# A decoder layer on one core: the second norm's rows in two halves, query units by token halves, and a new order of moves and stores

## The chip, the cores and the metric

The kernel runs on one core of a Trainium2 chip. The metric is the device time of one execution in microseconds (us); three runs of the kernel before gave a median of 809.94 us (808.97 to 810.89). About 0.2%, or 1.6 us, is what a measurement of this kernel can tell from no change.

## The reference, cut to what matters

Input x is 16 x 64 tokens of width 512, all in float32. Three steps follow each other, each with a residual:

```python
x = x + attn(layernorm(x))                    # scores over the 16 sequences, per channel; no weights
x = x + xattn(layernorm(x), ctx, mask, Wq, Wk, Wv, Wo, q_norm_w, k_norm_w)
        # 32 query heads of 128, 8 key/value heads: q = h @ Wq.T, k = ctx @ Wk.T, v = ctx @ Wv.T,
        # RMS norm of every q and k head, softmax(q k / sqrt(128) + mask) v, @ Wo.T
x = x + ffn(layernorm(x), ...)                # 16 experts, 4 per token, and a shared one
```

The change lies between the first and the second step: the second layer norm, the transposes of its rows, and the queries of the first of the eight head groups.

## The kernel before, in words

Every product is made of float16 halves: an operand is split into a high part (ScalarE, ACT, a copy to float16) and a low part (VectorE, DVE, or GpSimd, POOL, the difference), and TensorE (PE) adds high*high, high*low and low*high. So each result that feeds another product passes PE, ACT, then DVE or POOL, then PE again.

Time falls into a first stage (about the first 60 us: load x, first norm, attention over sequences), the eight head groups of the cross attention (about 62.7 us each once they run, to about 540 us) and the experts. A head group is software-pipelined: `iteration(i, att, proj)` does the attention of group i and the projections of group i+1. `iteration(-1, ...)`, the place of this change, has only projections: the queries of group 0, while keys and values of group 0 are made just before it. All order is written by hand; each engine works through its own list, and semaphores carry the waits.

Around the change, engine by engine:

- **DVE**: adds the first attention's result to x (L1238), takes statistics, computes the scale of each of 16 rows of 64 tokens (`row_scales`), then normalises 10 rows (L1193) while ACT normalises 6 (L751). Then 8 times `transposed_lo` (L1254), `v_lo_part` (L1264), and per query unit k of `iteration(-1)` a `q_lo_part` (L1279) and a `pre_lo` (L1364: low part of a 128x512 piece of expert weights, "units" 4 to 11). Between these stand `key_norm` (L1342, k = 1, 2), `key_lo` (L1348, k = 4, 5) and the second `v_lo_part` (k = 7).
- **ACT**: 8 times `transposed_hi` (L819), `v_hi_part` (L895), `k_scale(0)` (L877, L880), and per query unit `q_parts`: high part (L832), square (L836), high part of the square (L838), then `first_hi` (L924). `k_scale(1)` stands at k = 1, `k_hi_part` (L884) at k = 3, 4, the second `v_hi_part` at k = 7. After unit 7 come `wq_chunk` four times (L761), `q_rms` (L889, L891), which waits for the second half of the query squares' sums, `wkv_chunk`, four pairs of weight splits (L913, L915), and then `q_parts` of the next group.
- **PE**: first half of the values (L1742), 8 times `transpose_rows` (L1828, 4 transposes each), `sum_k_squares` (L1911, L1912), then 8 query units `project_q` of 12 products of 128x512; unit u is head u // 2 and token half u % 2. Unit u waits for `q_split` of unit u-2 (L1867), since two PSUM banks alternate. After unit 7 it computes the second half of the values (48 small products, 2.7 us), sums the query squares of the first token half (L1902, 32 products of one column) and goes on to group 0's scores (`scores`, L1844), which wait for all of `q_split` and for both `k_split` (L1847, L1848).
- **POOL**: `square_lo` per unit (L623), `k_square_lo` (L629), for which it waits until DVE's rows are normalised.
- **SyncE (SP)** issues the transfers: stores of split weights, second-round loads (L443), then four moves of x from one SBUF layout to another (L449), wq and wkv of group 1 (L421, L423), third-round loads (L402), stores of the second round (L416), wo (L460), stores of the third round, each followed by a load for group 1. `first_hi` of the third round (k = 4 to 7) waits on ACT for the store of the second round in the same slot (L922).

Of the kernel before, what the change touches and what calls it, by code (L numbers as in the profile page):

```python
# [18 lines left out]
ALU = mybir.AluOpType  # L19
# [55 lines left out]
DVE_ROWS = [n for n in range(B) if n not in ACT_ROWS]  # L75


def rows_to(rows, n):

    return sum(m <= n for m in rows)  # L80

# [12 lines left out]
def decoder_kernel(nc, x_half, ctx_t, mask, wq, wkv, wo, qk_norm, gate_t, bias, wgu, wd, h_rows, out):  # L94
    with ExitStack() as ctx:
# [292 lines left out]
        def _(sp):  # L388
# [55 lines left out]

            x_pairs = xh.rearrange("p (t b) l -> p t b l", b=2)
# [5 lines left out]
            query_weights(1)  # L451
            sp.wait_ge(hT_ps, NT)
            for q in range(SLOTS):
                sp.wait_ge(pre_in[q], 32)
                pre_load(0, 2 * SLOTS + q)
# [80 lines left out]
        def _(pool):  # L536
# [82 lines left out]
            def square_lo(p, u):  # L619
                j, th = u // 2, u % 2  # L620
# [53 lines left out]
            pool.wait_ge(h2_dve, len(DVE_ROWS))  # L674
# [52 lines left out]
        def _(act):  # L727
# [100 lines left out]
            def q_parts(p, u):  # L828
                j, th = u // 2, u % 2
# [87 lines left out]
            def first_hi(q):  # L917
# [3 lines left out]
                if n:  # L921
                    act.wait_ge(pre_stored[us], 16 * n)  # L922
# [15 lines left out]
            def iteration(i, att, proj, split):  # L938
# [4 lines left out]
                for k in range(8):  # L943
# [197 lines left out]
        def _(dve):  # L1141
# [43 lines left out]
            def normalise_rows(count, bank, dst, done):  # L1185
# [6 lines left out]
                for n in DVE_ROWS:  # L1192
                    dve.tensor_scalar(dst(n), xh[:, n, :], rstd[:, n:n + 1], shift_ln[:, n:n + 1],  # L1193
                                      ALU.mult, ALU.add).then_inc(done, 1)

            normalise_rows(1, 7, lambda n: hq[:, :, n], h1_dve)
# [73 lines left out]
            normalise_rows(2, 0, lambda n: h2[:, n, :], h2_dve)  # L1270
            for t in range(NT):
                transposed_lo(0, t, t % 4)
            v_lo_part(0, 0, 6)

            def q_lo_part(p, u):
                j, th = u // 2, u % 2
# [109 lines left out]
            def iteration(i, att, proj, split):  # L1386
# [4 lines left out]
                for k in range(8 if proj else 0):  # L1391
# [914 lines left out]
```

## Time and profile before

| what | value |
|---|---|
| runs shown | 808.97, 809.94, 810.89 us |
| profiled execution, its own time | 809.31 us |
| its span, first to last instruction | 807.5 us |
| PE busy | 777.2 us (96% of the span), 7887 matmuls |
| DVE, ACT, POOL busy | 591.6, 516.8, 543.3 us |
| mean granted TensorE clock | 0.993 |

A time line of the profile lists, for one engine, start, duration, line, output and inputs, count, and in brackets how long the engine stood idle before it and what released it. "x8" merges eight alike. Durations overlap the next start a little, since instructions are pipelined: a row of eight with 4.50 us is 0.56 us from start to start. PEclk 1.00 is the full 2.4 GHz, 0.50 is 1.2 GHz.

### The profile page before, as it was taken

What the parts mean: (1) busy time and instruction counts of PE and PEld (TensorE: products, weight loads), DVE (VectorE), ACT (ScalarE), POOL (GpSimd) and SP (SyncE); (2) the same over time, 40 slices, a digit from 0 to 9 for tenths busy, and PEclk for the clock granted to TensorE, in tenths of its full rate; (3) what the DMA queues carried; (4) which work ended last, traced back from release to release, by engine and by line L of the source; (5) the groups of instructions that cost most, each with busy time, mean ns of one, the idle gap of its engine ahead of it and who ended that gap; (6) DMA issues with size and microseconds to landing.
All of it is one profiled execution on the core that took longest, in us unless ns stands there. A gap on an engine that the chain in (4) does not pass through costs nothing.

```text
span 807.5 us, 21596 instructions
## 1 busy us (share of the span) xinstructions
PE 777.2 (96%) x7887; PEld 445.1 (55%) x7887; DVE 591.6 (73%) x1023; ACT 516.8 (64%) x968; POOL 543.3 (67%) x428
## 2 busy tenths in 40 slices
PE   6789999999999999999999999999998999999997
PEld 2664545645645655655654654654554565665653
DVE  5787795595685686777667668699688776767778
ACT  3898987487587587587578578636433566555551
POOL 6953496896896986976977978872253656565433
PEclk9799999999999999999999999999999999999999
DMA  8029516516507507516515524436515557678894
GB/s 329 18 95 290 164 67 235 143 53 227 165 26 234 164 18 238 168 36 229 158 55 188 176 79 151 124 113 248 177 52 209 199 182 248 219 282 277 264 401 183
DMA packets 50661, 138.94 MB, mean 172 GB/s; under 512 B 6176, under 2 KB 8224, under 8 KB 46240
## 3 DMA queue, kind: packets, MB, share of 16 engines
q1 hardware_dynamic: 43600, 116.93, 43.6%
q0 software_dynamic: 6400, 20.98, 7.6%
q8 instruction: 48, 0.79, 0.4%
q14 instruction: 21, 0.17, 0.1%
q10 hardware_dynamic: 592, 0.08, 0.1%
HBM read 96.02 MB, written 39.85 MB: 168 GB/s over the span
## 4 chain that ended last, share of the span: by engine, by line
PE 62%; POOL 13%; issue 8%; DVE 5%; DMA 5%; ACT 4%; SPq 2%; DVEq 0%; POOLq 0%; ACTq 0%
PE ps L1742 33%; PE ps L2192 18%; POOL ring_mem L623 4%; DMA stage<-in_wq 3%; POOL reg_h L661 3%; POOL ring_mem L609 2%; PE ps L2182 2%; POOL reg_h L665 2%; PE ps L1961 2%; POOL ring_mem L616 1%; PE ps L2253 1%; PE ps L1947 1%; PE ps L2207 1%; DMA w_split<-stage 1%; PE ps L1902 1%
## 5 line engine op out<-in xcount | busy, mean ns | idle before, releaser
L1742 PE MATMUL ps<-wo_hi,reg_b 128*128 128x512 f16 x448 | 142.5, 379 | 1.0 <-DVE x_res L1336 1.0
L2192 PE MATMUL ps<-ring_mem,reg_h 128*64 x480 | 116.6, 379 | 4.1 <-DVE kv L1639 2.3
L703 POOL DMA_INDIRECT y_rows<-reg_h,to_row x40 | 66.7, 1669 | 77.3 <-ACT reg_h L1115 71.6
L661 POOL TENSOR_SCALAR reg_h<-reg_h 128x512 f32<-128x512 f32 x56 | 95.4, 1704 | 33.2 <-ACT reg_h L913 33.0
L2194 PE MATMUL ps<-kv,reg_h 128*64 128x512 f16 x480 | 116.7, 380 | 0.0
L665 POOL TENSOR_TENSOR reg_h<-reg_h 128x512 f16<-128x512 f32 x84 | 108.7, 1294 | 4.7
L1742 PE MATMUL ps<-hT_hi,wq_hi 128*128 128x512 f16 x256 | 97.2, 380 | 2.0 <-DVE ring_mem L1279 1.8
L1742 PE MATMUL ps<-hT_hi,wq_lo 128*128 128x512 f16 x256 | 97.2, 380 | 0.0
L1742 PE MATMUL ps<-hT_lo,wq_hi 128*128 128x512 f16 x256 | 97.1, 379 | 0.0
L623 POOL TENSOR_TENSOR ring_mem<-kv,ring_mem 128x512 f16<-128x512 f32 x64 | 80.3, 1255 | 24.2 <-ACT ring_mem L838 24.2
L1742 PE MATMUL ps<-wo_lo,reg_b 128*128 128x512 f16 x224 | 85.0, 379 | 0.0
L2192 PEld LDWEIGHTS ps<-ring_mem,reg_h 128*64 128x64 f16 x480 | 48.3, 110 | 46.5 <-issue 15.0
L1742 PEld LDWEIGHTS ps<-wo_hi,reg_b 128*128 128x128 f16 x448 | 43.6, 97 | 50.8 <-issue 2.8
L1328 DVE TENSOR_TENSOR reg_b<-ps,reg_b 128x1024 f16<-128x1024 f32 x28 | 34.1, 1218 | 48.3 <-ACT reg_b L863 48.3
L1279 DVE TENSOR_TENSOR ring_mem<-ps,ring_mem 128x512 f16<-128x512 f32 x64 | 43.8, 685 | 29.0 <-ACT kv L836 28.3
L1336 DVE SCALAR_TENSOR_TENSOR x_res<-ps,x_res 128x512 f32<-128x512 f32 x64 | 43.7, 683 | 26.9 <-PE ps L1742 26.9
L913 ACT ACTIVATE reg_h<-reg_h 128x512 f16<-128x512 f32 x84 | 51.9, 620 | 11.6 <-DMA reg_h<-in_wgu 7.8
L2192 PE MATMUL ps<-ring_mem,wkv_st 128*64 x240 | 58.4, 379 | 0.9 <-ACT wkv_st L1107 0.8
L2194 PE MATMUL ps<-kv,wkv_st 128*64 128x512 f16 x240 | 58.4, 380 | 0.0
L609 POOL TENSOR_TENSOR ring_mem<-ring_mem,mask_sb 128x512 f32<-128x512 f32 x32 | 40.5, 1284 | 26.2 <-DVE ring_mem L1288 26.2
L699 POOL DMA_INDIRECT hT_hi<-h_rows,from_row x40 | 39.1, 979 | 19.7 <-issue 12.7
L832 ACT ACTIVATE ring_mem<-ps 128x512 f16<-128x512 f32 x64 | 38.1, 595 | 21.9 <-PE ps L1742 21.7
(343 smaller groups left out, 2019.2 us busy)
## 6 DMA issues: line engine op xcount, KB each, us to landing
ring_mem<-w_split SPq DMA_DIRECT2D x16, 1536.0 KB, 7.7
w_split<-reg_h SPq DMA_DIRECT2D x88, 256.0 KB, 2.1
reg_h<-in_wgu SPq DMA_DIRECT2D x58, 256.0 KB, 3.6
stage<-in_wq SPq DMA_DIRECT2D x8, 1024.0 KB, 8.9
stage<-in_wo SPq DMA_DIRECT2D x8, 1024.0 KB, 6.6
reg_h<-in_wd SPq DMA_DIRECT2D x30, 256.0 KB, 3.1
wkv_st<-in_wkv SPq DMA_DIRECT2D x8, 512.0 KB, 9.5
ring_mem<-in_x_half SPq DMA_DIRECT2D x8, 256.0 KB, 6.1
```

The source lines that it names most:

```text
L609: pool.tensor_tensor(t, t, mask_sb[:, :].unsqueeze(1).to_broadcast([P, 8, S]), ALU.add).then_inc(masked, 1)
L623: pool.tensor_tensor(sq_lo[:, j // 2, 8 * th:8 * th + 8, j % 2, :], sq32[:, u % 2, :].rearrange("p (b s) -> p b s", s=S), w, ALU.subtract) ...
L661: pool.tensor_scalar(st, st, WS, None, ALU.mult).then_inc(pre_scaled_pool, 1)
L665: pool.tensor_tensor(hl[:, 1, :], st, hl[:, 0, :], ALU.subtract).then_inc(pre_split, 1)
L699: pool.indirect_dma_start(h_slot[r % KC], None, h_rows, bass.IndirectOffsetOnAxis(ap=from_row[:, r - 1:r], axis=0)).then_inc(gathered[r % ...
L703: pool.indirect_dma_start(y_rows, bass.IndirectOffsetOnAxis(ap=to_row[:, r - 1:r], axis=0), y[r % 2], None).then_inc(scattered[r % 2], 16)
L913: act.activation(pre_hl[us][:, 0, :], pre_st[us], ACT.Copy, scale=WS).then_inc(pre_hi, 1)
L1279: dve.tensor_tensor(q_lo[:, j // 2, 8 * th:8 * th + 8, j % 2, :], ps[:, 4 + u % 2, :].rearrange("p (b s) -> p b s", s=S), q_hi[:, j // 2, ...
L1336: dve.scalar_tensor_tensor(x_res[:, t, :], ps[:, 2 + t % 2, :], 1.0 / (WS * WS), x_res[:, t, :], ALU.mult, ALU.add).then_inc(o_added, 1)
L1742: last = pe.matmul(dst, lhsT(c), rhs(c), start=(m == 0), stop=(m == n - 1))
L2192: pe.matmul(dst[0:TS, :], x[:, 0:TS], ring[:, bass.ds(at + w, BANK)], start=(first and n == 0), stop=(stop and n == 2))
L2194: last = pe.matmul(dst[TS:P, :], x[:, TS:P], upper_w[r % 2][:, w:w + BANK], start=(first and n == 0), stop=(stop and n == 2))
```

## The change

Rows of the second norm, their splits and transposes are taken in two halves of eight rows, with ACT and DVE going back and forth; PE computes the first query unit (head 0, first token half) between the two halves of the transposes; units of this group are then ordered (head 0, 1 of the first token half, head 0, 1 of the second, then heads 2 and 3 alike). The second half of the values, which ran after unit 7, is spread: one tile before the transposes, one after the first four, two after the last four. The sums of the key squares follow units 1 and 2. The key steps on ACT and DVE move to later units: `k_scale` to k = 2, 3, `key_norm` to 3, 4, `k_hi_part` to 5, 6, `key_lo` to 6, 7. SP issues group 1's wq and wkv and the third-round loads ahead of x's moves, and the third round's `first_hi` no longer waits for a store.

```diff
+SECOND_ACT_ROWS = ((1, 4, 6), (9, 12, 14))
+SECOND_DVE_ROWS = ((0, 2, 3, 5, 7), (8, 10, 11, 13, 15))
+def unit(p, u):
+    return (2 * (u // 4) + u % 2, u % 4 // 2) if isinstance(p, int) and p == 0 else (u // 2, u % 2)
...
# sync
+            query_weights(1)
+            sp.wait_ge(hT_ps, NT)
+            for q in range(SLOTS):
+                sp.wait_ge(pre_in[q], 32)
+                pre_load(0, 2 * SLOTS + q)
             x_pairs = xh.rearrange("p (t b) l -> p t b l", b=2)
             sp.wait_ge(x1_done, 8)
             ... four moves of x ...
-            query_weights(1)
-            sp.wait_ge(hT_ps, NT)
-            for q in range(SLOTS):
-                sp.wait_ge(pre_in[q], 32)
-                pre_load(0, 2 * SLOTS + q)
# gpsimd
-            pool.wait_ge(h2_dve, len(DVE_ROWS))
+            pool.wait_ge(h2_dve, len(SECOND_DVE_ROWS[0]))
# scalar
-                if n:
-                    act.wait_ge(pre_stored[us], 16 * n)
+                if n == 1:
+                    act.wait_ge(pre_stored[us], 16)
...
-                        if k == 1:
-                            k_scale(p, 1, 7)
-                        if k in (3, 4):
-                            k_hi_part(p, k - 3)
-                        if k == 7:
+                        if k in (2, 3):
+                            k_scale(p, k - 2, k - 2)
+                        if k in (5, 6):
+                            k_hi_part(p, k - 5)
+                        if k == 1:
                             v_hi_part(p, 1, 7)
...
-            normalise_rows(2, lambda n: h2[:, n, :], h2_act)
-            for t in range(NT):
-                transposed_hi(0, t, t % 4)
+            act.wait_ge(shift_ready, 2)
+            for part in range(2):
+                for n in SECOND_ACT_ROWS[part]:
+                    act.activation(h2[:, n, :], xh[:, n, :], ACT.Identity, scale=rstd[:, n:n + 1],
+                                   bias=shift_ln[:, n:n + 1]).then_inc(h2_act, 1)
+                for t in range(4 * part, 4 * part + 4):
+                    transposed_hi(0, t, t % 4)
             v_hi_part(0, 0, 6)
-            k_scale(0, 0, 7)
# vector: the same halves for its rows and transposed_lo, and
-                        if k in (1, 2):
-                            key_norm(p, k - 1)
-                        if k in (4, 5):
-                            key_lo(p, k - 4)
-                        if k == 7:
+                        if k in (3, 4):
+                            key_norm(p, k - 3)
+                        if k in (6, 7):
+                            key_lo(p, k - 6)
+                        if k == 1:
                             v_lo_part(p, 1, 7)
# tensor
+            def project_first_q():
+                pe.wait_ge(wq_split, KC)
+                pe.wait_ge(hT_hi_done, NT // 2)
+                ... for c in range(KC): wq_hi and wq_lo with hT_hi of the first half (8 products)
+                pe.wait_ge(hT_split, NT // 2)
+                ... for c in range(KC): wq_hi with hT_lo (4 products), then_inc(q_ps, 1)
...
-                            else:
-                                pe.wait_ge(hT_split, 4 * u + 4)
+                        if not att and u == 2:
+                            pe.wait_ge(hT_split, NT)
...
-                        project_q(p, u)
                         if not att and u == 0:
-                            pe.wait_ge(ln_k, 1)
-                            sum_k_squares(p, 1, 7)
+                            project_first_q()
+                            for t in range(NT // 2, NT):
+                                transpose_rows(t)
+                            project_v(0, 1, 7, range(2, 4))
+                        else:
+                            project_q(p, u)
+                        if not att and u in (1, 2):
+                            pe.wait_ge(hT_split, NT // 2 + u)
+                            sum_k_squares(p, u - 1, u - 1)
...
                     else:
-                        pe.wait_ge(ln_k, 2)
-                        project_v(p, 1, 7)
                         sum_q_squares(p, 3, range(NT // 2))
...
+            pe.wait_ge(x1_done, 4)
+            project_v(0, 1, 7, range(1))
             pe.wait_ge(var_ready, 2)
-            for t in range(NT):
+            for t in range(NT // 2):
                 transpose_rows(t)
-            sum_k_squares(0, 0, 7)
+            project_v(0, 1, 7, range(1, 2))
             iteration(-1, False, True)
```

## Rows read from the trace of the kernel before

**Rows 1.** The page's first part: busy time and share of each engine.
```profile
PE 777.2 (96%) x7887; PEld 445.1 (55%) x7887; DVE 591.6 (73%) x1023; ACT 516.8 (64%) x968; POOL 543.3 (67%) x428
```

**Rows 2.** Busy time in one stretch: us, busy us (instructions) per engine, PEclk, DMA share, GB/s.
```profile
300.00:400.00 100.00, 99.88 (x846) 55.55 (x844) 70.65 (x97) 70.68 (x125) 81.36 (x60) 1.00 0.51 162
```

**Rows 3.** PE in order of time: start, us, line, form, count [idle before <-releaser].
```profile
57.70 2.11 PE L1828 MATMUL ps<-ident,reg_h 128*128 128x128 f32 x16 [1.67 <-DVE reg_h L1193]
61.36 0.90 PE L1828 MATMUL ps<-ident,reg_h 128*128 128x128 f32 x5 [1.56 <-DVE hT_lo L1254]
...
84.29 0.39 PE L1742 MATMUL ps<-hT_hi,wq_hi 128*128 128x512 f16 x1 [0.83 <-DVE ring_mem L1279]
...
86.89 0.22 PE L1742 MATMUL ps<-wkv_hi,ring_mem 128*128 128x128 f16 x1
...
89.57 0.94 PE L1902 MATMUL ps<-ones,ring_mem 128*128 128x1 f16 x32
90.37 0.86 PE L1742 MATMUL ps<-kv,ring_mem 128*128 128x64 f16 x24
...
99.89 0.39 PE L1742 MATMUL ps<-hT_hi,wq_hi 128*128 128x512 f16 x1 [0.57 <-DVE ring_mem L1279]
```

**Rows 4.** ACT in order of time, second norm to the next head group; same columns.
```profile
56.95 3.06 ACT L751 ACTIVATE reg_h<-ring_mem,shift_ln,rstd 128x256 f32<-128x256 f32 x6 [0.31 <-DVE shift_ln L1189]
59.92 4.50 ACT L819 ACTIVATE hT_hi<-ps 128x512 f16<-128x512 f32 x8
...
64.79 0.69 ACT L877 ACTIVATE kv<-ps,eps_ln 128x512 f32<-128x512 f32 x1
...
66.84 0.60 ACT L832 ACTIVATE ring_mem<-ps 128x512 f16<-128x512 f32 x1 [0.70 <-PE ps L1742]
...
81.31 0.63 ACT L924 ACTIVATE reg_h<-reg_h 128x512 f16<-128x512 f32 x1 [1.49 <-DMA w_split<-stage]
...
87.09 0.60 ACT L832 ACTIVATE ring_mem<-ps 128x512 f16<-128x512 f32 x1 [0.32 <-PE ps L1742]
...
88.74 0.61 ACT L924 ACTIVATE reg_h<-reg_h 128x512 f16<-128x512 f32 x1
...
90.26 2.18 ACT L761 ACTIVATE wq_hi<-stage 128x512 f16<-128x512 f32 x4
92.34 0.27 ACT L889 ACTIVATE rq<-ps,eps_q 128x32 f32<-128x32 f32 x1
```

**Rows 5.** DVE in order of time, the same stretch.
```profile
56.95 3.32 DVE L1193 TENSOR_SCALAR reg_h<-ring_mem,rstd,shift_ln 128x256 f32<-128x256 f32 x10
60.53 4.88 DVE L1254 TENSOR_TENSOR hT_lo<-ps,hT_hi 128x512 f16<-128x512 f32 x8 [0.26 <-ACT hT_hi L819]
...
82.59 0.68 DVE L1348 TENSOR_TENSOR kv<-kv 128x512 f16<-128x512 f32 x1
...
88.28 0.69 DVE L1279 TENSOR_TENSOR ring_mem<-ps,ring_mem 128x512 f16<-128x512 f32 x1 [0.23 <-ACT kv L836]
89.39 1.23 DVE L1364 SCALAR_TENSOR_TENSOR reg_h<-reg_h 128x512 f16<-128x512 f32 x1 [0.42 <-ACT reg_h L924]
```

**Rows 6.** SyncE's queue in order of time: the four moves of x.
```profile
58.44 5.78 SPq L449 DMA_DIRECT2D x_res<-ring_mem  x4
```

**Rows 7.** Stretches with PE idle and the clock around them, columns as in rows 2.
```profile
21.31:23.18 1.87, 0.00 (x1) 0.00 (x0) 0.67 (x1) 1.31 (x2) 1.87 (x2) 1.00 0.03 13
...
24.90:28.30 3.40, 3.40 (x70) 2.78 (x71) 3.15 (x6) 2.44 (x5) 3.40 (x2) 0.50 0.00 0
32.93:36.18 3.25, 0.01 (x1) 0.04 (x1) 3.11 (x6) 3.15 (x7) 3.25 (x2) 0.84 0.00 0
...
35.10:41.95 6.85, 5.78 (x48) 5.81 (x50) 5.20 (x10) 6.36 (x11) 3.28 (x2) 0.50 0.01 4
...
610.60:613.15 2.55, 0.20 (x8) 0.04 (x3) 2.34 (x5) 1.08 (x3) 0.94 (x1) 1.00 0.55 231
```

**Rows 8.** PE in order of time, the longest stall between 200 and 500.
```profile
265.27 0.38 PE L1742 MATMUL ps<-wo_hi,reg_b 128*128 128x512 f16 x1 [0.71 <-DVE x_res L1336]
```

More of the change, by code:

```diff
@@ L75, with second_rows_to @@
 DVE_ROWS = [n for n in range(B) if n not in ACT_ROWS]
+SECOND_ACT_ROWS = ((1, 4, 6), (9, 12, 14))
+SECOND_DVE_ROWS = ((0, 2, 3, 5, 7), (8, 10, 11, 13, 15))
 def rows_to(rows, n):
     return sum(m <= n for m in rows)
+def second_rows_to(rows, n):
+    return max(i + 1 for i, m in enumerate(itertools.chain(*rows)) if m <= n)
+def unit(p, u):
+    return (2 * (u // 4) + u % 2, u % 4 // 2) if isinstance(p, int) and p == 0 else (u // 2, u % 2)
 def sums_to(t, k=None):
@@ L619, in square_lo @@
             def square_lo(p, u):
-                j, th = u // 2, u % 2
+                j, th = unit(p, u)
                 pool.wait_ge(sq_hi_done, ev(p, 8, u))
@@ L828, in q_parts @@
             def q_parts(p, u):
-                j, th = u // 2, u % 2
+                j, th = unit(p, u)
                 bank = ps[:, 4 + u % 2, :]
@@ L1183, in _, with row_shifts @@
             row_scales(1, 7)
-            def normalise_rows(count, bank, dst, done):
+            def row_shifts(count, bank):
                 dve.wait_ge(rstd_ready, count)
@@ L1191, in normalise_rows, with normalise_row @@
                 dve.wait_ge(shift_ready, count)
[L1192 to L1196, printed above, removed]
+            def normalise_row(n, dst, done):
+                dve.tensor_scalar(dst, xh[:, n, :], rstd[:, n:n + 1], shift_ln[:, n:n + 1],
+                                  ALU.mult, ALU.add).then_inc(done, 1)
+            row_shifts(1, 7)
+            for n in DVE_ROWS:
+                normalise_row(n, hq[:, :, n], h1_dve)
             dve.memset(used[:, 0:PRE], 1.0)
@@ L1269, in _ @@
             then(dve.tensor_tensor(wqk[:, :], norm_sb[:, 0:1], norm_sb[:, 1:2], ALU.mult))
-            normalise_rows(2, 0, lambda n: h2[:, n, :], h2_dve)
-            for t in range(NT):
-                transposed_lo(0, t, t % 4)
+            row_shifts(2, 0)
+            for part in range(2):
+                for n in SECOND_DVE_ROWS[part]:
+                    normalise_row(n, h2[:, n, :], h2_dve)
+                for t in range(4 * part, 4 * part + 4):
+                    transposed_lo(0, t, t % 4)
             v_lo_part(0, 0, 6)
             def q_lo_part(p, u):
-                j, th = u // 2, u % 2
+                j, th = unit(p, u)
                 dve.wait_ge(q_hi_done, ev(p, 8, u))
@@ L1819, in transpose_rows @@
             def transpose_rows(t):
-                pe.wait_ge(h2_dve, rows_to(DVE_ROWS, 2 * t + 1))
-                pe.wait_ge(h2_act, rows_to(ACT_ROWS, 2 * t + 1))
+                pe.wait_ge(h2_dve, second_rows_to(SECOND_DVE_ROWS, 2 * t + 1))
+                pe.wait_ge(h2_act, second_rows_to(SECOND_ACT_ROWS, 2 * t + 1))
                 if t >= 4:
@@ L1862, in project_q @@
             def project_q(p, u):
-                j, th = u // 2, u % 2
+                j, th = unit(p, u)
                 if u == 0:
@@ L1873, in project_q @@
                         range(KC)).then_inc(q_ps, 1)
+            def project_first_q():
+                pe.wait_ge(wq_split, KC)
+                pe.wait_ge(hT_hi_done, NT // 2)
+                for c in range(KC):
+                    for w in (wq_hi, wq_lo):
+                        pe.matmul(ps[:, 4, :], w[:, c, 0:HD], hT_hi[:, c, 0:BANK], start=(c == 0 and w is wq_hi), stop=False)
+                pe.wait_ge(hT_split, NT // 2)
+                for c in range(KC):
+                    last = pe.matmul(ps[:, 4, :], wq_hi[:, c, 0:HD], hT_lo[:, c, 0:BANK], start=False, stop=(c == KC - 1))
+                last.then_inc(q_ps, 1)
             def project_k(p, th):
@@ L2077, in _ @@
             project_v(0, 0, 6, range(2, 4))
+            pe.wait_ge(x1_done, 4)
+            project_v(0, 1, 7, range(1))
             pe.wait_ge(var_ready, 2)
-            for t in range(NT):
+            for t in range(NT // 2):
                 transpose_rows(t)
-            sum_k_squares(0, 0, 7)
+            project_v(0, 1, 7, range(1, 2))
             iteration(-1, False, True)
```

## The prediction

> **What bounds the kernel now.** I read the page's busy times first, then a table of busy time by stretches, then the time lines of PE, ACT, DVE and SyncE around the change. PE is busy for 777.2 of 807.5 us [rows 1] and for 99.88 of 100 us in the middle of the head groups [rows 2], so a microsecond that PE gains or loses before them arrives at the end almost whole. The longest stall between 200 and 500 us is 0.71 us [rows 8]. Ahead of the head groups PE does stand still: 1.67 us before the second norm's transposes, 1.56 us in the middle of them, 0.83 us before query unit 7, 0.57 us before unit 2 of the next group [rows 3]. The first two are what the halves are aimed at. The second thing to see is that ACT is as full there as PE: from 66.84, when it takes unit 0, to 87.09, when it takes unit 7, it idles for little but a 1.49 us wait for a store [rows 4]. Each query unit passes PE, ACT, DVE, and PE may run only two units ahead.
>
> **The change part by part.** Nothing moves before 56.95, when ACT and DVE begin their rows [rows 4, 5].
>
> *First half.* ACT takes 0.51 us a row (3.06 / 6) and 0.56 a high part (4.50 / 8) [rows 4]; DVE 0.33 a row and 0.61 a low part [rows 5]. After three rows ACT starts its four high parts at about 58.4; the last starts at 60.1 and PE sees it at 60.8. PE meanwhile does one value tile (0.67: a quarter of the 2.68 us between 86.89 and 89.57 [rows 3]), so its first stall shrinks from 1.67 to 1.1, then come the first 16 transposes from 57.7 (2.1 us [rows 3]) and another value tile, and waits 0.3 us. The first query unit runs from 60.8 to 63.4 instead of from 64.05.
>
> *Second half.* The last 16 transposes follow at 63.4 (they need DVE's row 15, ready at 63.2) and take 2.1 to 2.3 us, then two value tiles, 1.34: PE starts unit 1 at 67.0. It has most of its two stalls back, but has spent them on value tiles and on a unit that ACT cannot take yet. For ACT can make the second half's high parts only as the transposes come: it idles from 62.2 to 64.0, ends them at 66.4, does a value split, and **takes unit 0 at about 66.85, against 66.84 before** [rows 4]. This is the step that decides: the halves gain ACT nothing.
>
> *ACT from there to unit 7.* A unit with its weight split takes 1.65 + 0.52 = 2.17 us (87.09 to 88.74; 2.08 / 4) [rows 4]. Seven of them are 15.2. Both `k_scale` now lie here (before, one lay ahead of unit 0, at 64.79): about 1.3 each, 2.6. Two key high parts 1.0, one value split 0.5. Waits for PE: 0.8 before unit 1 (taken at 69.8, 2.8 after PE starts it), 0.4 before unit 2. The wait of 1.49 for the store [rows 4] is gone, since the third round has buffers of its own; the wait for its load replaces it at no cost, being issued at about 66, some 15 us ahead. Sum 20.5: unit 7 is taken at 87.3, against 87.09. The cover for all removed waits was ACT work, and that work is now the path.
>
> *After unit 7.* PE ends unit 7 at about 86.9 in both. Before, 2.68 us of values followed, then 0.8 us of sums, and the scores began at 90.37 without a stall [rows 3]. Now the values are used up. The scores need `q_split` of unit 7 and both `k_split`, and DVE has `key_lo(1)` last in its list, behind the weight split of k = 7, which waits for ACT's. From ACT's 87.3: 1.65 to its weight split (88.95), 0.65 to DVE's (88.74 to 89.39 [rows 4, 5]), 1.15 for that, about 0.75 for `key_lo` [rows 5]: the keys are ready at 91.5, or 91.3 with the shorter durations that these rows also allow. I take **91.4: PE stands still for about 3.6 us between 86.9 and 91.4, with 0.8 us of sums of one column in the middle, and starts the scores 1.0 us later than before.** ACT's `q_rms` needs the sums behind the first scores; it moves from 92.34 to about 93.1, +0.8, and with it the next group's first `q_parts`. There PE had 0.57 us of stall [rows 3], so its +1.0 is no more than ACT's +0.8. Net at this point: **+0.8**, between +0.3 (every DVE row at its shortest) and +1.2.
>
> *DVE and POOL share.* DVE's last weight split took 1.23 us [rows 5], while `key_lo`, of the same shape, took 0.68 with POOL idle. The Trainium skill (SBUF — State Buffer, "SBUF: two separate sides") has DVE operations with two SBUF inputs and POOL operations lock each other out for a whole instruction, and POOL's square split of unit 7 would still run there. By that rule the price is 1.23 again and the sum stays; without it the split would take 0.68 and the scores would come 0.5 us sooner, +0.3 to +0.5. The trace agrees with the rule, so I keep 1.23.
>
> *Queues.* SP issues group 1's wq and wkv at 58.4 instead of behind the 5.78 us of x's moves [rows 6]; neither is needed before 89. The third-round loads wait for the last transpose (65.7), the moves then run to about 73.5, and the second-round stores behind them start less than 1 us later. x's new place is first read after 94. I cost all of it at nothing; if a third-round load came late, ACT would wait again, at most the old 1.49. POOL's key squares start 1.6 us earlier, which nobody waits for.
>
> **The clock.** A stretch of some 4.4 us in which PE does only 0.8 us of one-column sums is new. In this trace a stall of 3.25 us (32.93 to 36.18) brought the granted clock down to 0.50 within it, and it stayed there until 41.95; one of 1.87 us with 64x32 products around it was followed by 3.40 us at 0.50; one of 2.35 us among full-width products left it at 1.00 [rows 7]. The new one is longer than all that were harmless, so I expect PE at 1.2 GHz behind it. The price is half of the time that PE works at the low level: 1.7 us from the 3.40 us stretch, 2.9 from 36.18 to 41.95. I take their mean, 2.3. PE would be ready for unit 2 of the next group at 99.3 + 1.0 + 2.3 = 102.6 instead of starting it at 99.89: +2.7, less what the low clock does not stretch (waits for weights of one-column sums, at most 0.4): **+2.5**, between +1.9 and +3.1.
>
> **Sum.** The profiled execution took 809.31 us (span 807.5, 1.8 around it). 809.31 + 2.5 = 811.8. It lies 0.6 under the median of the three runs; by the median it would be 812.4. I give 812.1. About 0.2% or 1.6 us is what a measurement of this kernel can tell from no change.
>
> **The rivals.**
>
> *The clock holds* (not slower). Then only the +0.8 stays: 810.1 by the profile, 810.7 by the median. For it: the 2.35 us stall [rows 7], and that sums and scores alone, which the old trace has from 89.57 on [rows 3], did not lower it. Against: 3.25 us did. It decides if the stall comes out under some 2.5 us.
>
> *The tail is short, ACT's waits count.* If the keys were ready with `q_split` (about 89.2), the scores would start 1.2 us earlier and `q_rms` at about 91.5: -0.8, limited by ACT's list, so 808.5. To be faster by more than 0.2% the 0.71 us stall at 265.27 [rows 8] would have to go too: 807.8. Against it stands the order in the diff.
>
> *The stores or loads pile up* behind x's moves, so that group 1's pieces are late for ACT at 94: up to 1.5 us on top of the +0.8, 811.6 to 812.4. Little speaks for it: before, the moves stood ahead of the same transfers.
>
> *The change does not do what it says*: the wait for the store could come back as one for the load in the same slot; 1.49 us of ACT, the same time as above.
>
> **How the numbers follow.** Clock falls 0.46; clock holds 0.34; short tail 0.12, of which 0.08 beyond 0.2%; pile-up or returned wait 0.08, half of it beyond 0.2%. Faster 0.08, slower 0.50, same 0.42. The likeliest case alone reaches from 811.2 to 813.0. The range takes in the clock-holds case with its lower bound (809.31 + 0.3) and some spread above: 809.7 to 813.4.
>
> **What would show it.** Right: PE's first unit near 60.8; ACT idle 1.8 us before its fifth high part and at unit 0 near 66.9; no wait for a store at k = 4; a PE stall of about 3 us before the first scores, released by DVE L1348's counterpart; then granted clock 0.5 for 3 to 6 us. Wrong: scores that start at or before 90.4, ACT's unit 0 before 66, or full clock behind the stall.

## The result and the profile after

The kernel after took 813.49 us (median of 20 runs, 810.28 to 818.40), beside 810.25 us for the kernel before in the same session (20 runs): a ratio of 1.0042, 95% interval 1.0031 to 1.0054. So it is slower, by 2.5 to 4.4 us. Forecast were 812.1 us and a range up to 813.4: the direction was right, the size too small (+2.2 us to the 809.94 of the runs shown, against +3.2 by the medians and +3.4 by the ratio). The profiled execution took 812.29 us, 2.98 more than the one of before.

The page's first part for the kernel after; PE is busy 2.5 us longer with the same 7887 products [rows 1], which is a sign of a lower clock:

```profile
PE 779.7 (96%) x7887; PEld 448.5 (55%) x7887; DVE 593.0 (73%) x1023; ACT 516.4 (64%) x968; POOL 543.9 (67%) x428
```

PE in order of time, columns as in [rows 3]:

```profile
58.37 1.94 PE L1849 MATMUL ps<-ident,reg_h 128*128 128x128 f32 x16 [1.60 <-DVE reg_h L1209]
61.29 0.38 PE L1901 MATMUL ps<-hT_hi,wq_hi 128*128 128x512 f16 x1 [0.31 <-ACT hT_hi L831]
...
87.42 0.95 PE L1934 MATMUL ps<-ones,ring_mem 128*128 128x1 f16 x32 [0.24 <-POOL ring_mem L635]
91.49 1.44 PE L1763 MATMUL ps<-kv,ring_mem 128*128 128x64 f16 x24 [3.12 <-DVE kv L1369]
92.73 1.02 PE L1934 MATMUL ps<-ones,ring_mem 128*128 128x1 f16 x32
...
102.07 0.38 PE L1763 MATMUL ps<-hT_hi,wq_hi 128*128 128x512 f16 x1
```

The stall of 1.56 us in the middle of the transposes is gone, that of 0.83 has become 0.55 us (at 81.50), and in their place stands one of 3.12 us ahead of the scores, released by DVE L1369, `key_lo`. ACT and DVE over the same stretch, as in [rows 4, 5]:

```profile
57.63 1.58 ACT L1055 ACTIVATE reg_h<-ring_mem,shift_ln,rstd 128x256 f32<-128x256 f32 x3 [0.31 <-DVE shift_ln L1204]
64.52 2.06 ACT L831 ACTIVATE hT_hi<-ps 128x512 f16<-128x512 f32 x4 [1.91 <-PE ps L1849]
66.92 0.64 ACT L844 ACTIVATE ring_mem<-ps 128x512 f16<-128x512 f32 x1
...
87.21 0.60 ACT L844 ACTIVATE ring_mem<-ps 128x512 f16<-128x512 f32 x1
...
93.79 0.29 ACT L901 ACTIVATE rq<-ps,eps_q 128x32 f32<-128x32 f32 x1 [2.23 <-PE ps L1934]
```

```profile
88.43 0.68 DVE L1300 TENSOR_TENSOR ring_mem<-ps,ring_mem 128x512 f16<-128x512 f32 x1
89.51 1.23 DVE L1385 SCALAR_TENSOR_TENSOR reg_h<-reg_h 128x512 f16<-128x512 f32 x1 [0.40 <-ACT reg_h L936]
90.66 0.68 DVE L1369 TENSOR_TENSOR kv<-kv 128x512 f16<-128x512 f32 x1
```

The last query unit is split at 89.1; the keys are ready only at 91.3, since the weight split stands ahead of them. Busy time by stretches shows the clock, columns as in [rows 2]:

```profile
89.30:90.00 0.70, 0.00 (x0) 0.00 (x0) 0.49 (x1) 0.70 (x3) 0.70 (x1) 0.58 0.80 269
90.00:96.00 6.00, 4.51 (x102) 4.54 (x103) 4.86 (x8) 3.73 (x9) 0.19 (x1) 0.50 0.99 356
96.00:97.00 1.00, 1.00 (x32) 0.98 (x30) 1.00 (x3) 1.00 (x3) 0.14 (x1) 0.88 0.07 27
```

The clock falls to 1.2 GHz within the stall and stays there for 6.8 us (twice 1 minus the clock, times the length, summed over the three rows). The first 24 score products take 1.44 us instead of 0.86 [rows 3].

**A common start for the marks.** Repeats show that the second norm's rows start at 56.4 to 58.8 us by chance, whatever the kernel. So the marks, in the text and in the table, are in us from that start (56.95 before, 57.63 after); times in the rows of a profile are from the start of the span. Three marks matter: the first scores, ACT's `q_rms`, and PE's unit 2 of the next group, from which on PE runs almost without a stall. Before: 33.42, 35.39 and 42.94. After: 33.86, 36.16 and 44.44.

### The profile page after: what moved, and what is told of

Read it like the earlier page. It is cut to its first block, busy times and chain, and to the rows that moved or that the text cites. A ratio compares the mean times of both kernels' runs of the same rounds, so it can differ in the third digit from the quotient of the medians.

```text
span 810.5 us, 21594 instructions
## 1 busy us (share of the span) xinstructions
PE 779.7 (96%) x7887; PEld 448.5 (55%) x7887; DVE 593.0 (73%) x1023; ACT 516.4 (64%) x968; POOL 543.9 (67%) x428
## 4 chain that ended last, share of the span: by engine, by line
PE 81%; ACT 5%; DVE 5%; DMA 5%; issue 2%; POOL 1%; DVEq 0%; SPq 0%; POOLq 0%; ACTq 0%
PE ps L1763 52%; PE ps L2230 14%; DMA y_rows<-reg_h,to_row 4%; PE ps L1993 3%; PE ps L1979 2%; PE ps L2220 2%; PE ps L1934 1%; PE ps L2291 1%; PE ps L2245 1%; DMA ring_mem<-in_x_half 1%; PE ps L1780 1%; POOL ring_mem L621 1%; PE ps L1806 1%; PE ps L1815 1%; PE ps L2232 1%
## 5 line engine op out<-in xcount | busy, mean ns | idle before, releaser
L1763 PE MATMUL ps<-hT_hi,wq_hi 128*128 128x512 f16 x252 | 95.5, 379 | 0.7 <-DVE ring_mem L1300 0.6
L1763 PE MATMUL ps<-hT_hi,wq_lo 128*128 128x512 f16 x252 | 95.5, 379 | 0.0
```

The lines of the kernel that those rows point to most:

```text
L1763: last = pe.matmul(dst, lhsT(c), rhs(c), start=(m == 0), stop=(m == n - 1))
```

## The experiments

All ratios are to the kernel before on the same chip, with 12 runs of each variant. `after +` means that the edit was made in the kernel after. "Keys first", "old queues" and the like are explained below the table. Marks are from one profiled execution each, ratios from all runs, and the two need not agree to better than the 1.1 to 2.1 us that an interval reaches to either side.

| run | ratio [95% interval] | first scores | unit 2 of the next group | us at 1.2 GHz around the scores |
|---|---|---|---|---|
| before, again | 0.9994 [0.9974, 1.0013] | 33.21 | 42.73 | 0 |
| after, again | 1.0039 [1.0018, 1.0060] | 33.84 | 44.91 | 6.8 |
| after + keys first | 1.0012 [0.9994, 1.0031] | 32.21 | 43.27 | 3.4 |
| after + held clock | 1.0023 [1.0007, 1.0039] | 33.85 | 43.41 | 0 |
| after + two value tiles last | 1.0021 [0.9999, 1.0043] | 32.86 | 43.14 | 3.4 |
| after + keys first and held clock | 1.0003 [0.9981, 1.0025] | 33.70 | 44.15 | 0 |
| after + old queues | 1.0026 [1.0008, 1.0043] | 33.99 | 45.16 | 6.8 |
| before + late keys | 1.0026 [1.0004, 1.0048] | 34.15 | 43.38 | 0 |
| before + new queues | 1.0001 [0.9984, 1.0017] | 32.42 | 43.03 | 0 |
| before + no wait for stores | 0.9986 [0.9965, 1.0008] | 32.41 | 42.60 | 0 |
| the same, wo behind unit 0 | 0.9988 [0.9971, 1.0006] | 32.41 | 41.92 | 0 |
| the same, wo behind the scores | 1.0001 [0.9984, 1.0018] | 33.87 | 43.38 | 0 |
| that, and the experts' clock held | 0.9987 [0.9974, 1.0000] | 32.41 | 41.94 | 0 |
| after + both clocks held | 0.9999 [0.9980, 1.0019] | 35.12 | 44.36 | 0 |
| after + key scale in ACT's gap | 1.0008 [0.9982, 1.0034] | 32.17 | 42.50 | 0 |
| that, SP's old order | 0.9996 [0.9976, 1.0017] | 32.18 | 42.62 | 0 |

**Both kernels again.**

> The kernel before, once more, for a second profile of it and the scatter of the comparison: ratio 1.000 within 0.2%. If the changed kernel's profile owed part of its 3.0 us to chance, this profile starts the second norm later than 56.95 us (at 57.5 to 58.0, as the four experiments did) and shows the granted clock at 0.50 behind the experts' 2.35 us stall near 613, so that its span is 809 to 811 us. If not, it repeats 807.5 us.

> The changed kernel, once more, on the same chip as the others: ratio to the kernel before 1.003 to 1.005, a stall of about 3.1 us before the first scores released by the key's low part, and the granted clock at 0.50 for 3 to 7 us behind it. If the fall of the clock was chance, this profile shows 1.00 there.

The loss came again (1.0039), and so did its picture: 3.10 us of stall ahead of the scores.

**Keys first.** DVE's list in the kernel after, with `key_lo` ahead of the weight split:

```diff
                     if not att:
+                        if k in (6, 7):
+                            key_lo(p, k - 6)
                         pre_lo(SLOTS + k)
...
-                        if k in (6, 7):
-                            key_lo(p, k - 6)
```

> The changed kernel with one move: DVE makes the key's low part ahead of the weight split in k = 6 and 7, not behind it. Theory (the scores wait for the last item of DVE's list, and the wait brings the clock down): the stall before the first scores falls from 3.1 us to 1.0 to 1.6 us and is now released by the query split of unit 7; the granted clock stays at 1.00 from 85 to 100 us; the time lies 2.5 to 4 us under the changed kernel, at -0.3 to -1 us to the kernel before. Rival (the loss comes from the queues' order or from the halves themselves): the time stays within 1 us of the changed kernel, 2 to 3 us above the kernel before.

PE in order of time in this variant:

```profile
88.30 0.95 PE L1934 MATMUL ps<-ones,ring_mem 128*128 128x1 f16 x32 [0.76 <-POOL ring_mem L635]
90.20 0.86 PE L1763 MATMUL ps<-kv,ring_mem 128*128 128x64 f16 x24 [0.95 <-DVE kv L1369]
91.13 0.95 PE L1934 MATMUL ps<-ones,ring_mem 128*128 128x1 f16 x32
91.94 2.72 PE L1763 MATMUL ps<-kv,ring_mem 128*128 128x64 f16 x48
95.22 0.93 PE L1763 MATMUL ps<-kv,ring_mem 128*128 128x64 f16 x24 [0.56 <-issue]
```

The scores begin 1.65 us sooner than in the kernel after, still released by `key_lo` (L1369), and the ratio falls from 1.004 to 1.0012. That is less than was expected, since the clock fell all the same, though the stalls are only 0.76 and 0.95 us with the sums between, but later (91.9) and for half as long. The last line shows something new: the profile marks the stall "issue", PE waits for nothing that it knows. I read that as instructions that come late, and come back to it.

**Held clock.** Twelve products that nobody reads, behind the query squares' sums:

```diff
                         sum_q_squares(p, 3, range(NT // 2))
+                        for _ in range(12):
+                            pe.matmul(ps[:, 2, :]..., ident16[:, :], blockmask16[:, :]..., start=True, stop=True)
```

> The changed kernel with 12 extra full-width products (2.6 us, their result is not used) behind the first sums of query squares, where PE otherwise stands still; nothing else moves, the scores still start when the keys are ready. Theory (the low clock behind the stall is a cost of its own, 1.5 to 2.9 us): clock 1.00 from 85 to 100 us, first scores again near 91.4, q_rms at 93.0 instead of 93.8, time 1 to 2.5 us under the changed kernel and 0.5 to 1.2 us above the kernel before. Rival (the low clock is hidden by ACT, which limits the next units): within 0.5 us of the changed kernel.

```profile
88.58 2.75 PE L2064 MATMUL ps<-blockmask,ident 128*128 128x512 bf16 x12
91.83 0.86 PE L1763 MATMUL ps<-kv,ring_mem 128*128 128x64 f16 x24 [0.50 <-DVE kv L1369]
92.52 0.94 PE L1934 MATMUL ps<-ones,ring_mem 128*128 128x1 f16 x32
93.33 2.33 PE L1763 MATMUL ps<-kv,ring_mem 128*128 128x64 f16 x72
```

The scores begin where they did (33.85), at full speed, and unit 2 comes at 43.41 instead of 44.73 (mean of four profiles of the kernel after): **the fallen clock is worth 1.3 us** by the marks, and 1.3 to 1.5 us by the ratios (1.0023 against 1.0039 and 1.0042). The mean clock over the runs rose from 0.987 to 0.993.

**Two value tiles last.** The third and fourth value tile back behind unit 7, as cover for the wait (`project_v(0, 1, 7, range(2, 4))` moved, and its splits on ACT and DVE back to k = 7).

> The changed kernel with the last two of the four value tiles back behind query unit 7 on PE (1.34 us), and their splits back at k = 7 on ACT and DVE. Theory: PE starts units 1 to 7 up to 0.5 us earlier but ACT still sets their pace; the stall before the scores shrinks by about 1.3 us to 1.8 us, the scores start at 91.4 as before since the key split is still last, and the clock stays at 1.00; time 1 to 2 us under the changed kernel, 0.8 to 1.8 above the kernel before. Rival (a stall of under 2 us with the sums around it is still enough to bring the clock down): no gain, within 0.5 us of the changed kernel.

The stall is 2.20 us instead of 3.12, the clock low for 3.4 us instead of 6.8, the ratio 1.0021. The clock did not hold as the theory had it, but with two tiles of cover it is low for half as long in this profile.

**Keys first and held clock**, both edits at once.

> After, with both of two earlier edits: key_lo ahead of the weight splits, and 12 products of full width behind the query squares' sums, which nobody reads. Theory (late keys and the fallen clock are the whole of the first stage's loss): the clock stays at 1.00 from 50 to 130, the mean clock over the runs is that of the kernel before (0.992), ratio 1.000 with at most 0.0015 to either side. Rival (the halves themselves, or the queues, cost something else besides): the clock holds and the ratio is still 1.002 or more.

1.0003, as expected, and the mean clock of the runs (0.992) no lower than that of before (0.991). The rival is excluded only in part, since the interval reaches 1.0025. The profile does not confirm it: the 12 products run until 91.3, so they are now themselves what the scores wait for (33.70), 0.89 us of issue stall follow, and unit 2 comes at 44.15, 1.3 us later than before. By the ratio the loss is gone, by this one profile's marks it is not.

**Old queues.** The kernel after with SyncE's old order and the waits for stores.

> The changed kernel with the queues as before (x's moves ahead of wq, wkv and the third-round loads; the third round waits for stores). Theory (halves and the late key split make the loss, the queues' part gives ACT 1.5 us and takes it back in later transfers): ACT waits 0.5 to 1.5 us for a store near 81, the scores start 0.5 to 1.5 us later than at 91.5, time within 1 us of the changed kernel or up to 1.5 above it. Rival (the new order of the queues, which b1 showed to hold up PE's instructions at 95, makes a good part of the loss): time 1 to 2 us under the changed kernel.

Still slower (1.0026), with the same stall (2.95 us) and low clock: most of the loss is not in the queues. The ratio lies 1.1 us under that of the kernel after on this chip (1.0039), the medians are alike (815.76 and 815.80 us), so a small part for the queues is not excluded. ACT's wait for a store is only 0.20 us here.

**Late keys alone**, in the kernel before: `key_lo` at k = 6, 7 behind the weight split, all else as it was, so the values still follow unit 7.

```diff
-                        if k in (4, 5):
-                            key_lo(p, k - 4)
+                        if k in (6, 7):
+                            key_lo(p, k - 6)
```

> The kernel before with one edit: DVE's key_lo stands at k = 6, 7 behind the weight splits instead of at k = 4, 5, and the values still follow unit 7 on PE. Theory (the late keys alone cost about 1 us of scores, and the clock falls only since the spread values no longer fill the wait): the scores start about 1.0 us later against the start of the rows, PE's stall there is 1 to 1.5 us and not 3, the granted clock stays at 1.00 behind it, ratio 1.0005 to 1.0015. Rival (the late keys are the whole loss): the clock falls here too and the ratio is 1.003 to 1.004.

PE stands still for 0.86 us and the clock holds:

```profile
92.39 0.86 PE L1742 MATMUL ps<-kv,ring_mem 128*128 128x64 f16 x24 [0.86 <-DVE kv L1348]
...
91.00:93.00 2.00, 1.14 (x44) 1.08 (x41) 2.00 (x4) 2.00 (x5) 0.09 (x1) 1.00 1.05 398
93.00:97.00 4.00, 4.00 (x118) 3.48 (x115) 4.00 (x8) 3.36 (x8) 0.00 (x0) 1.00 0.35 119
```

Scores 0.8 us later and unit 2 0.55 us later than the means of the two profiles of before (33.32, 42.83). That is the first half of the theory. The ratio, 1.0026 or 2.1 us, is more than these marks explain, though its interval begins at 1.0004, and the mean clock of the twelve runs is 0.989 against 0.991 for the kernel before: that the clock held is shown for this one profile, and in some of the other runs it may have fallen.

**The queues alone**, in the kernel before: the new order on SyncE and no wait for stores in the third round.

> The kernel before with only the change of the queues: wq, wkv and the third-round loads ahead of x's moves, and no wait for a store in the third round. Theory (the queues' part is harmless): the 1.49 us wait of ACT is gone, PE's 0.83 us before unit 7 too, the scores start 0.8 to 1.2 us earlier than at 90.37, time -0.5 to -1.2 us to the kernel before. Rival (the order of the queues makes part of the loss, through later stores, wo or group 1's loads): time above the kernel before by 0.5 us or more, with an ACT wait for a load or for wo after 88 us.

**No wait for stores alone**, SyncE's order as before:

```diff
-                if n:
-                    act.wait_ge(pre_stored[us], 16 * n)
+                if n == 1:
+                    act.wait_ge(pre_stored[us], 16)
```

> The kernel before with one edit: the third round of first_hi no longer waits for a store; SyncE's order stays. Theory (the change in the queues as a whole came out at zero because late PE instructions behind denser traffic gave back what ACT's gone wait had brought): here ACT's wait of 1.3 to 1.5 us near 82 and PE's 0.83 us stall before unit 7 are gone, the scores start about 0.8 us sooner against the start of the second norm's rows, there is no stall of kind issue at 95, and PE reaches the next group 0.6 us sooner: ratio 0.9985 to 1.0. Rival (PE's stalls before unit 7 are hidden by another wait, whatever the traffic): unit 2 of the next group is as late as before and the ratio is 1.000; a stall of kind issue here too would say that the order of the transfers is not what makes PE's instructions late.

In both, ACT's wait and PE's 0.83 us stall are gone and the scores begin 0.9 us sooner. And in both most or all of it is given back within the scores: unit 2 comes at 43.03 and 42.60, against 42.83. PE, before + new queues first, then before + no wait for stores, with the busy table of the latter:

```profile
95.11 0.84 PE L1742 MATMUL ps<-kv,ring_mem 128*128 128x64 f16 x23 [1.66 <-issue]
```

```profile
91.34 1.59 PE L1742 MATMUL ps<-kv,ring_mem 128*128 128x64 f16 x49
94.17 0.84 PE L1742 MATMUL ps<-kv,ring_mem 128*128 128x64 f16 x23 [1.24 <-issue]
...
90.00:92.00 2.00, 2.00 (x79) 2.00 (x76) 2.00 (x5) 2.00 (x5) 0.00 (x0) 1.00 1.06 398
92.00:94.00 2.00, 0.93 (x32) 0.81 (x28) 2.00 (x4) 1.97 (x6) 0.00 (x0) 1.00 0.95 362
```

The 16 DMA engines are full (1.06, 0.95) just when PE runs through a hundred small products in 3 us. The profile lists a queue of its own for instructions among the transfers, here for the stretch from 88 to 96 us (packets, MB, share):

```profile
q8 instruction: 2, 0.03, 1.6%
```

The kernel before has the same two packets there and no such stall; what differs is when the first of them is moved. In all 20 profiles this queue moves one packet of 0.02 MB near the scores. In the six with an issue stall it starts 1.2 to 2.6 us behind the first scores, and PE goes on 2.3 to 2.4 us after its start. In the other fourteen it starts between 0.7 us ahead of the first scores and 0.8 us behind them, and no issue stall follows. That PE waits for this packet is read from this order in time; no run moved the packet alone.

**Is it the transfers?** The 1 MB load of wo(0) moved away from that stretch, behind the first query unit of group 1:

```diff
-            sp.dma_start(wo_st, wo[0]).then_inc(wo_in, 16)
             for q in range(2 * SLOTS, UNITS):
                 first_store(q)
                 pre_load(1, q - 2 * SLOTS)
+            sp.wait_ge(q_ps, 9)
+            sp.dma_start(wo_st, wo[0]).then_inc(wo_in, 16)
```

> The kernel before without the wait for stores in the third round, and with the load of wo(0) moved on SyncE from ahead of the last stores and loads (83.4 us) to behind them and behind the first query unit of group 1 (about 97). Theory (PE's instructions come late because the transfers of 84 to 95 fill the DMA engines): the transfers end near 92, there is no stall of kind issue over 0.3 us in the scores, PE reaches the next group about 1.2 us sooner than without the move of wo; ACT may wait for wo at 100 for 0.5 to 1.5 us, of which at most half arrives. Ratio 0.997 to 0.999. Rival (the stall of kind issue belongs to a place in PE's program or to the dense row of small products, whatever the transfers): it is there again with 1 us or more, and the ratio is 0.9986 or, with ACT's wait, 1.000.

```profile
91.55 2.26 PE L1743 MATMUL ps<-kv,ring_mem 128*128 128x64 f16 x72
...
90.00:92.00 2.00, 2.00 (x80) 2.00 (x77) 2.00 (x4) 2.00 (x5) 0.00 (x0) 1.00 0.58 199
92.00:94.00 2.00, 2.00 (x64) 1.84 (x61) 2.00 (x5) 1.97 (x6) 0.00 (x0) 1.00 0.46 133
...
101.31 0.63 ACT L937 ACTIVATE wo_hi<-stage 128x512 f16<-128x512 f32 x1 [1.93 <-DMA stage<-in_wo]
```

With the DMA share at half, the 72 products run through, and the instruction packet starts 33.1 us behind the rows' start, instead of 34.5 with wo's load in its old place. Unit 2 starts at 41.92, 0.9 us sooner than in the kernel before. But ACT waits 1.93 us for wo, and 1.43 us of that come back as a PE stall at 103.8. The load belongs between the two:

> The kernel before without the wait for stores in the third round, and with the load of wo(0) behind the end of group 0's scores (about 94). Theory (the transfers of 84 to 95 make PE's instructions late, and ACT needs wo only at 99.6): no stall of kind issue over 0.3 us in the scores, wo lands by 98, ACT does not wait for it over 0.3 us, unit 2 of the next group starts 0.9 us sooner against the rows' start than before, ratio 0.997 to 0.999. Rival: wo still comes late for ACT or the stall of kind issue is back with part of the traffic; then the ratio is 0.9985 to 1.000.

> As the kernel beside it, with 10 products of full width that nobody reads ahead of the experts' stall of 2.35 us near 613. Theory (that stall brings the clock down in two executions of three, for 3 us at 0.50, 1.7 us of time): the clock stays at 1.00 from 100 to 808, ratio 0.001 to 0.002 lower than beside it, 0.995 to 0.998. Rival (PE's low clock there is hidden by another engine): the ratio is that of the kernel beside it.

With the load behind the scores (`sp.wait_ge(s_ps, 4)`) there is neither issue stall nor wait for wo. In the first profile the clock fell in the second norm's own stall and was low from 60 to 67, which moved all marks by about 1.5 us. The second shows what was expected, unit 2 at 41.94. The 10 products ahead of the experts' stall keep the clock there, and the ratio is 0.9987 [0.9974, 1.0000], 1.1 us under its neighbour's median. Three versions without the halves lie together at the front (0.9986, 0.9988, 0.9987), about 1 us faster than before, and none of them is clear of no change. So what the move of wo gains at unit 2 (0.7 us against no wait for stores alone) is not seen in the ratios.

**The experts' clock in the kernel after.** In 12 of the 18 profiles in which nothing fills it, of all kinds of variants, the experts' stall of 2.35 us near 613 was followed by 3.4 us at 1.2 GHz. Here 12 unread products stand behind the query squares' sums and 10 ahead of that stall.

> After with 12 products of full width, which nobody reads, behind the query squares' sums, and 10 of them ahead of the experts' stall of 2.35 us near 613. Theory (what after loses beyond the late keys is clock, part of it behind the experts' stall): the granted clock stays at 1.00 from 50 to 808, the mean clock over the runs is 0.995 or more, and the ratio is 1.000 within 0.0015. Rival (the clock of the experts is not part of it): mean clock up as well, ratio still that of the variant with the first dozen alone, 1.002.

The clock was full behind both stalls, and the ratio 0.9999 [0.9980, 1.0019]. This profile's first scores come late (35.12), since its clock fell in the second norm's stall. The mean clock over the runs is 0.991 and not 0.995: falls ahead of the changed stretch remain.

**Where else is the clock low?** Two more profiles of the kernel after.

> After once more, one look for its granted clock. Its mean clock over the runs is 0.986, while the two profiled executions so far showed 0.987 and 0.989. Theory (every execution loses the clock in the first scores, some again behind the experts' stall, and a few for longer in the scores): 5 to 7 us at 0.50 from about 90, and where the mean clock is 0.985 or less, 3 us more near 614. Rival (the further loss lies in another place): low clock in a stretch that neither profile of after showed.

> As the look before it: the same kernel, for the stretches of low clock in one more execution, with the same two theories.

They took 813.21 and 812.01 us with stalls of 3.11 us ahead of the scores; the first of them by stretches:

```profile
91.30:98.00 6.70, 5.35 (x117) 5.38 (x118) 5.55 (x10) 4.43 (x10) 0.06 (x1) 0.52 0.90 324
617.00:621.00 4.00, 4.00 (x44) 2.35 (x40) 2.62 (x7) 0.97 (x2) 0.00 (x0) 0.57 0.04 11
```

All four profiles of the kernel after have 6.8 us at the low clock here; neither profile of the kernel before has any. The other low stretches (23 to 30, 36 to 43, 615 to 620) stand in profiles of before too, some at other lengths or times (12 to 17 instead of 23 to 30). So the rival does not hold.

**Can the halves pay?** ACT's gap of 1.9 us between the halves filled with the first key's scale, the key steps a unit or more earlier and ahead of the weight splits, two value tiles last; then the same with SyncE's old order. Of the edit only the first part is shown.

```diff
+                if part == 1:
+                    k_scale(0, 0, 5)
                 for t in range(4 * part, 4 * part + 4):
                     transposed_hi(0, t, t % 4)
```

> A version to beat both: the changed kernel with the first key scale (1.3 us of ACT) put into ACT's 1.9 us of idle time between the halves, the key's low parts ahead of the weight splits and one unit earlier, and the last two value tiles behind unit 7 to cover PE. Theory: ACT takes unit 7 about 1.2 us earlier, the scores start at 88.6 to 89.5, the clock stays at 1.00, time 1 to 2 us under the kernel before. Rival (PE's gain is given back by instructions or loads that arrive late, as at 95 us in b1 and a1, since transfers are not earlier): a stall of 1 to 3 us at 93 to 96 put down to issue, time within 0.7 us of the kernel before.

> The variant with one key scale in ACT's gap, keys first and the last two value tiles last, with SyncE's old order of transfers, still without the wait for stores in the third round. Theory (its stall of kind issue at 93, 0.81 us, comes from the moves and stores that the new order pushes to later): the scores start as soon as there (about 32 us after the rows' start), no stall of kind issue over 0.3 us in them, q_rms 34.5 us or less after the rows' start, ratio 0.998 to 1.000. Rival (PE's instructions come late whatever the order, whenever the scores start that early): the stall is there again, and the ratio is that of the variant, 1.001.

The scores begin at 32.2 and the clock holds, but DVE, now ahead of ACT with the keys, delays query units (a PE stall of 1.65 us before unit 7, behind a second `key_norm` that takes 1.73 us instead of 0.74), and issue stalls cost 0.81 and 1.09 us. The ratios 1.0008 and 0.9996 are no change. The order of SyncE's transfers does not decide on the issue stalls; so that part of the theory falls.

## Why the prediction was right and wrong

- **Halves.** PE's first unit starts 3.66 us behind the rows (forecast 3.85), ACT's gap is 1.91 us (1.8). Right.
- **"The halves gain ACT nothing", then a sum of 20.5 us to unit 7.** ACT takes unit 0 at 9.29 us behind the rows instead of 9.90 (its last four high parts took 1.9 us and not 2.4), and unit 7 at 29.58 instead of 30.35 (before: 30.14). The step was 0.8 us too dear, but its conclusion holds at unit 7: with only the wait for stores gone and no halves, ACT takes it at 29.13, and with the halves and the old queues at 29.74, against 30.14 and 29.93 in the two profiles of before. So what ACT gains there comes from the removed wait, and the halves with the moved key steps take back 0.4 us of it.
- **Keys last in DVE's list.** Right in kind and place: PE stands still for 3.4 us in all (3.6), released by `key_lo`. DVE's weight split took the 1.23 us assumed, beside POOL's last square split (89.03 to 90.19), and `key_lo`, with POOL idle, 0.68. The rule of the Trainium skill cited in the prediction (SBUF — State Buffer, "SBUF: two separate sides") agrees with that. The closer comparison is the weight split itself, which took 0.69 us at 81.98 in the kernel before, with POOL idle. The scores come 0.5 us later than before, not 1.0, because unit 7 was earlier.
- **`q_rms` +0.8.** Measured +0.77, but out of two errors that cancel: half from the late scores, half from score products and sums at the low clock.
- **Clock falls.** Right, and for a little more than the 3 to 6 us: 6.8 us. Its price of 2.3 us, taken from stretches in which PE was busy throughout, was too high: 1.3 us by the held clock, since PE idles in 2.1 of the 6.8 us, the one-column sums hardly stretch (1.02 us instead of 0.94) and the next group had 0.57 us of slack.
- **Net at unit 2.** Forecast +2.5 us. The four profiles give 44.44, 44.91, 44.88 and 44.68, mean 44.73, against 42.83 in the two of before: **+1.9 us**.
- **Queues "at nothing".** Right for the sum (1.0001 alone) but for a wrong reason: the gone wait for stores is worth 0.9 us at the scores, and issue stalls of PE take it back. That mechanism was in none of my cases.
- **The sum.** This is the step that failed: everything outside the marked stretch, behind unit 2 above all, was put at nothing. Unit 2 explains 1.9 us, less than the 2.5 forecast, and the ratios say 3.3 (3.4 and 3.2; 2.5 to 4.4 in the first comparison): about 1.4 us stand in no term. That the forecast came as near as it did owes something to luck, since the clock's price was too high by 1.0 us and this term too low by 1.4.
- **What the runs show of those 1.4 us.** The profiles do not place them: from unit 2 to the end it is 708.4, 710.2, 707.7 and 708.4 us in the kernel after and 707.6 and 711.3 in before, a scatter greater than what is sought. The profiled executions of the kernel after also lie under its medians (812.29, 813.39, 813.21, 812.01 against 813.49 and 815.80). The mean clock accounts for a part: over all runs it is 0.986 to 0.987 against 0.991 to 0.992 for before, and 0.005 of 810 us is 4 us lost to the clock, of which the 6.8 low microseconds are 3.4. So 0.6 us of clock are lost elsewhere. Among the 20 runs of the kernel after, one with 0.001 less mean clock (0.8 us lost) took about 0.4 us longer, so I estimate 0.3 us of time for them. The rest, about 1 us, stays open.
- **The absolute time.** 813.49 lies 0.1 us above the range. The session alone is more than that: the kernel before itself was 0.3 us slower than in the runs shown. And 812.1, midway between 811.8 and 812.4, took 0.3 us off the forecast difference.

Which part costs what, by the experiments: without the key wait the loss falls from 3.3 us to 1.0; with the clock held to 1.9; with both to 0.2. Those are shown by the ratios, each within 1.3 to 1.8 us; only the last is clear of the kernel after's own interval. That the spread values set the clock free to fall rests on one profile each of late keys with the old values (clock holds) and of two tiles moved back (half as long); it is likely, not shown.

## What to carry to other kernels

Work that stands behind the last unit of a stage is cover for its tail: before spreading it into earlier stalls, look at which operand the next stage waits for and where that stands in each engine's list, because a few stalls of 1 us scattered among wide products cost less than one of 3 us that also takes the clock. Fill a gap only if the engine behind it can take the result; PE's regained microseconds here went into a unit that ACT could take only 0.6 us sooner, and seven units later nothing of it was left. And when a removed wait brings nothing, look for "issue" stalls beside a full DMA share, and for the packets of the instruction queue: a load moved by some ten microseconds took the stall away here, though its gain was too small for the ratios.

## What the runs showed of the hardware

- PE stood still for 0.56 to 1.66 us with the mark "issue" in six variants, always among the 72 small score products of group 0 (PE goes on at 93.2 to 95.2 us), with a DMA share of 0.96 to 1.04 just ahead; it did not where wo's load was moved and the share was 0.46 to 0.65. A full share is not enough: the kernel before passes the same place at 1.05 and 0.82 without a stall. What tells the two kinds apart in all 20 profiles is the packet of the instruction queue: over 1.1 us behind the first scores with the stall, at most 0.8 us behind them without.
- Stalls of 0.76 and 0.95 us with one-column sums between brought the clock down (keys first); one of 0.86 us behind values and sums did not (late keys alone). A stall of 2.35 us did in 12 of 18 profiles, and the second norm's stall, where it was 1.9 to 2.6 us, in four of nine; where it was 0.7 to 1.7 us, in none of eleven. The same stall has both outcomes. The low clock behind them measured 3.4 or 6.8 us each time, with nothing between.
- The place and length of the low clock vary from run to run and move the mean clock of one kernel between 0.985 and 0.998, so that by my estimate a change of 1 us needs tens of runs: 12 runs against 23 or 35 left intervals of 1.1 to 2.1 us to either side.
